# GpSimd instead of SyncE waits at the program's end for the semaphores of the last stores

## The reference

```python
# attention: 16 heads of 16 features; within one token, feature i of Q against feature j of K
Q = (x @ Wq.T).reshape(b, length, 16, 16).swapaxes(-2, -1)      # K, V likewise from the context
qk = jnp.einsum('blih,bljh->blij', Q, K) / sqrt(16)
attn = softmax(qk, axis=-1)
valued = jnp.einsum('blij,bljh->blih', attn, V)                  # back to 256 features, @ Wo.T

x = x + tanh(g_xattn[0]) * xattn(layernorm(x), ctx)
# feed forward: 8 experts, each token takes the one with the largest gate
idx = argmax(softmax(xf @ Wg + bg))
y_e = gelu(xf @ W1[e] + b1[e], exact) @ W2[e] + b2[e]
x = x + tanh(g_ffn[0]) * y_idx                                   # xf is layernorm(x)
```

## Time and profile before

| What | Value |
|---|---|
| median of 3 runs | 300.7 us (300.69 to 301.26) |
| the profiled execution's own time | 300.25 us |
| its span, first to last instruction | 298.4 us |
| what lies around the span | 1.85 us |
| mean granted TensorE clock | 0.988 of full |
| PE busy | 279.1 us (94% of the span) |
| DVE busy | 209.5 us (70%) |
| POOL busy | 130.3 us (44%) |
| ACT busy | 105.3 us (35%) |

### The profile page before, as it was taken

How to read it: one execution, slowest core, us unless ns; L and a number is a source line. 1 busy time by engine, 2 the same in 40 slices (tenths; PEclk the granted TensorE clock), 3 DMA queues, 4 the chain that set the end, 5 groups by cost and what they waited for, 6 DMA issues and landing times.

```text
span 298.4 us, 9824 instructions
## 1 busy us (share of the span) xinstructions
PE 279.1 (94%) x3181; PEld 216.9 (73%) x3182; DVE 209.5 (70%) x611; ACT 105.3 (35%) x258; POOL 130.3 (44%) x157
## 2 busy tenths in 40 slices
PE   7989999999999999999999999968788999999970
PEld 6558677677776776767767777857677999999960
DVE  6576586696785875978668678867588766666650
ACT  2021321303213113032130320355555777877730
POOL 9512041243624525336154352722757555445551
PEclk9999999999999999999999999999999999999995
DMA  7666255464674746637646643423334544344210
GB/s 264 197 196 162 67 141 146 122 218 139 194 194 132 221 128 210 216 96 218 189 146 208 178 130 107 123 73 90 110 113 152 162 142 131 97 133 117 85 56 0
DMA packets 30955, 43.25 MB, mean 145 GB/s; under 512 B 7629, under 2 KB 17998, under 8 KB 30928
## 3 DMA queue, kind: packets, MB, share of 16 engines
q1 hardware_dynamic: 17872, 21.48, 25.9%
q10 hardware_dynamic: 9648, 12.86, 14.3%
q0 software_dynamic: 3408, 8.59, 8.2%
HBM read 24.83 MB, written 10.60 MB: 119 GB/s over the span
## 4 chain that ended last, share of the span: by engine, by line
PE 75%; DVE 8%; SPq 5%; issue 3%; DMA 2%; POOL 2%; ACT 1%; DVEq 1%; ACTq 1%; POOLq 0%
PE ps_pr L397 17%; PE ps_qo L405 16%; PE ps_so L430 8%; PE ps_av L451 8%; PE ps_tr L599 5%; PE ps_av L611 4%; PE ps_so L599 4%; PE ps_to L611 4%; PE ps_tr L439 3%; PE ps_pr L587 2%; PE ps_to L464 2%; SPq L318 2%; SPq L326 2%; DMA sb_wkv<-wkv_in 2%; ACTq L318 1%
## 5 line engine op out<-in xcount | busy, mean ns | idle before, releaser
L397 PE MATMUL ps_pr<-sb_wkv,sb_ct 128*128 128x512 f32 x128 | 62.1, 609 | 0.8 <-DMA sb_wkv<-wkv_in 0.5
L659 ACT ACTIVATE sb_pe_x<-sb_pe_x 128x512 f32<-128x512 f32 x16 | 10.1, 631 | 112.0 <-DVE sb_pe_x L817 112.0
L1247 POOL TENSOR_SCALAR sb_ve<-sb_mv 128x2 f32<-128x2 f32 x16 | 3.5, 220 | 88.1 <-DVE sb_mv L786 84.5
L397 PEld LDWEIGHTS ps_pr<-sb_wkv,sb_ct 128*128 128x128 f32 x128 | 22.5, 189 | 20.5 <-issue 19.9
L802 DVE STREAM_TRANSPOSE sb_y_q<-sb_q_n 128x512 f32<-128x512 f32 x16 | 17.4, 1090 | 26.8 <-ACT sb_q_n L654 26.8
L1262 POOL DMA_INDIRECT routed_rows<-sb_xs,sb_pos_i x32 | 32.5, 1016 | 8.3 <-issue 7.7
L405 PE MATMUL ps_qo<-sb_wog,sb_ot 128*128 128x264 f32 x128 | 31.4, 388 | 1.1 <-ACT sb_ot L670 1.1
L405 PEld LDWEIGHTS ps_qo<-sb_wog,sb_ot 128*128 128x128 f32 x128 | 24.1, 190 | 11.2 <-issue 6.2
L430 PE MATMUL ps_so<-sb_kb,sb_y_q 128*32 128x128 f32 x1024 | 31.0, 273 | 0.5 <-DVE sb_y_q L802 0.5
L451 PE MATMUL ps_av<-sb_vb,sb_at 128*32 128x128 f32 x1024 | 31.3, 274 | 0.0
L451 PEld LDWEIGHTS ps_av<-sb_vb,sb_at 128*32 128x32 f32 x1024 | 27.0, 110 | 5.0 <-issue 5.0
(11 more groups left out here) (143 smaller groups left out, 481.4 us busy)
## 6 DMA issues: line engine op xcount, KB each, us to landing
sb_kb<-sb_y_k SPq DMA_DIRECT2D x124, 32.0 KB
sb_vb<-sb_y_v SPq DMA_DIRECT2D x124, 32.0 KB
sb_ct<-ctx_in ACTq DMA_DIRECT2D x15, 256.0 KB, 3.0
sb_x<-x_in ACTq DMA_DIRECT2D x15, 256.0 KB, 3.5
sb_xt<-xt_in_ ACTq DMA_DIRECT2D x14, 256.0 KB, 5.1
sb_xb<-routed_rows SPq DMA_DIRECT2D x25, 134.0 KB, 2.1
sb_w_all<-w_in_ SPq DMA_DIRECT2D x4, 514.0 KB
sb_w<-w_in SPq DMA_DIRECT2D x4, 512.0 KB
```

The source lines that it names most:

```text
L397: last = pe.matmul(pr[:, s * 512:(s + 1) * 512], lhsT=ct[i][:, kc, s, :], rhs=wkv[:, kc, :], start=(kc == 0), stop=(kc == KC - 1))
L659: act.activation(pe_x[:], pe_x[:], ACT.Exp, scale=float(H) ** -0.5).then_inc(exp_done, 1)
```

## The change

The loop that waits for the four `stored` semaphores is taken out of SyncE's stream and put at the end of GpSimd's, behind the last store. It is written there with `wait_apart`, so that each wait also increments the counter `passed_pool`. The values waited for are the same.

```diff
@@ -385,8 +385,6 @@
             sp.wait_ge(routed, 32 * pairs)
             sp.wait_ge(pad_in, 16 * E // 2)
             block_slots(sp, fetch, 0)
-            for i in range(OUT):
-                sp.wait_ge(stored[i], 16 * ((blocks + OUT - 1 - i) // OUT))
@@ -1308,6 +1306,8 @@
                     for q in range(2):
                         route(2 * (last_batch % 2) + q, last_batch)
             block_slots(pool, store, 0)
+            for i in range(OUT):
+                wait_apart(pool, stored[i], 16 * ((blocks + OUT - 1 - i) // OUT), passed_pool)
```

## The result

| | before | changed |
|---|---|---|
| median of 20 runs | 300.69 us | 302.06 us |
| ratio | | 1.0047, 95% interval 1.003 to 1.0065 |
| the profiled execution's own time | 300.25 us | 302.24 us |
| its span | 298.4 us | 300.4 us |
| mean granted TensorE clock | 0.988 | 0.987 |

The changed kernel is slower by 0.47%; the forecast was 302.0 us and +1.3 us. One of its 20 runs took 332.09 us at a granted clock of 0.847 and is left out of the ratio; the median of the other 19 is 301.99 us, 1.30 us above that of before.

What follows compares the result with a forecast made beforehand. The end was taken as bound by GpSimd's last store, its DRAIN and the release. DRAIN start 293.6 plus 5.88 plus 0.24 gives 299.7 against 298.4, +1.3 us: 300.7 + 1.3 = 302.0 us, range 300.4 to 303.2.

Steps and rivals of the forecast that it cites:

- The path at the end: At the span's end: GpSimd's last store, its DRAIN of 7084 ns on line 97, then the release of all engines.
- The removed part at 0.0: On SyncE: losing its four waits is worth 0.0 us, being covered by GpSimd's own DRAIN.
- The start of the DRAIN: On GpSimd behind the new waits: landing seen at 293.4, plus 0.2 us, so the DRAIN starts at 293.6.
- The bounds of 293.5 and 293.7: Earliest and latest start forecast for GpSimd's final DRAIN behind the new waits, around 293.6.
- 5.88 us that come with the DRAIN: At GpSimd's end: 5.88 us are work the DRAIN brings with it, starting when it reaches the idle engine.
- third rival: GpSimd's DRAIN waits for the last packet, then works 5.06 us: slower by only 0.5 us, 301.2 us; chance 10%.
- No price for handing over: Between GpSimd's waits and DRAIN: handing the DRAIN to the idle engine costs a tenth at most, not 0.7 us.
- The upper bounds of +2.0 and +2.5: GpSimd's end: +2.0 if up to 0.73 us issue time is exposed, +2.5 if all 7.08 us follow 293.6.
- The faster rival: GpSimd's DRAIN is long from polling for outstanding stores; after the landing it takes 0.17 us: 296.3 us; chance 17%.
- The rival of no change: GpSimd's 5.88 us run on by themselves after the last store, so the DRAIN ends at 298.16: 300.7 us; chance 13%.
- cleaning up after all 71 indirect DMAs: Example given, within the no-change case, of work GpSimd's cores might still do after the last store's record ends.

Runs made afterwards that it cites:

- experiment 4: Kernel before with one DRAIN added on GpSimd in its idle stretch while it waits for VectorE, 24 indirect DMAs issued by then; 305.69 us, ratio 0.9921.
- experiment 5: Kernel before, SyncE keeping the waits, with GpSimd DRAINs added in the idle stretch and behind stores 12, 23, 31 and 33; 297.25 us, ratio 0.9868.
- experiment 6: Kernel before, SyncE keeping the waits, with GpSimd DRAINs added only in the idle stretch and behind stores 23 and 31; 296.47 us, ratio 0.9838.
- experiment 8: Changed kernel with SyncE's four waits put back, so both engines wait; 301.85 us against 300.51, ratio 1.0038.
- experiment 2: Changed kernel with a GpSimd memset of 3.5 us between the four waits and the DRAIN; 313.87 us, one run, on a chip where before takes 308.39 us.
- experiment 7: The DRAINs of experiment 5 combined with the waits on GpSimd as in the changed kernel; 297.76 us, ratio to before 0.9891.
- experiment 1: Changed kernel with a second GpSimd DRAIN right behind the four waits; 310.18 us, one run, on a chip where before takes 308.39 us.

## Why the prediction was right

- **The path at the end.** Store, DRAIN, release was the reading of the earlier trace rows. Experiments 4 to 6 confirm it from the other side: with only the DRAIN shortened, the span ends earlier by what it lost (2.0 us in experiment 4), until the landing takes over: in experiment 5 it sets the end through SyncE's drain.
- **The removed part at 0.0.** Right (experiment 8).
- **The start of the DRAIN, 1.3 us behind the last store's end.** Right to the tenth: 1.33 in the changed kernel. The bounds of 293.5 and 293.7 for the start correspond to 294.2 and 294.4 there, and it is 294.28.
- **5.88 us that come with the DRAIN.** Right in size (5.874) and shown as a mechanism by experiment 2. In the kernel before they began as soon as the store had left the engine, at 292.28, while the store was still landing; SyncE's wait lay beside them. The change puts wait and work in a row, and the 1.3 us of the wait are the loss. That none of the 5.88 us was a wait for the landing was an assumption of the forecast; its third rival was the case without it. It held for this DRAIN with its 71 DMAs; in experiments 5 and 6 the DRAINs with 21 DMAs or fewer behind a store took 0.5 to 1.4 us more than the line.
- **No price for handing over.** The upper bounds of +2.0 and +2.5 were not needed: the last wait starts at 294.2 and the DRAIN at 294.3, and the DRAIN is no longer than 5.87. That the forecast of 302.0 us and the median of 302.06 meet so closely is in part luck: the interval of the ratio runs from +0.3% to +0.65%, 0.9 to 2.0 us.
- **The faster rival**, that the DRAIN waits for open transfers: false in the changed kernel, where all had landed and it took 5874 ns. A landing does lengthen a DRAIN that has few DMAs to account for (1.4 us with 5 in experiment 5, against 0.45 in experiment 7, where all had landed), but that is not where the 5.9 us come from. The figure of some 12 ns in the Trainium skill (VectorE: DVE Perf Modes, The DRAIN you can't avoid) is for the drains of the runtime's preamble and postamble; the one on line 97 closes the kernel's own block, so the prediction took the figure further than the page does. GpSimd comes near it only where it has issued no DMA since its last DRAIN: 34 ns in experiment 1.
- **The rival of no change**, work going on by itself: excluded by experiment 2. The Trainium skill says in Perfetto Trace Analysis, DMA Instruction — SWDGE (GPSIMD), that the processor completes the instruction after its record has ended. No run here shows how much later; it is not where the 5.88 us are.
- **The third rival**, work starting at the landing, 5.06 us long: excluded by the DRAIN's length after everything had landed, 5.87 us.
- **What the prediction did not know** is what the work is. It left "cleaning up after all 71 indirect DMAs" as an aside to a rival. The work does grow with that count, only it is done at another time: when the DRAIN runs, not before. That did not touch the forecast, since both kernels issue the same 71.

## What to carry to other kernels

When an engine's DRAIN ends a program, look at what it does after the engine has become idle, and let waits lie beside that work on another engine rather than ahead of it. On GpSimd that work grew here with the indirect DMAs since its last DRAIN, so a DRAIN in an idle stretch in the middle takes part of it off the end. A DRAIN added near the end needs enough stores behind it for the engine to catch up: seven were enough in experiment 6, and with five behind the last of two such DRAINs experiment 5 was still late by 0.75 us.

## What the runs showed of the hardware

- In these kernels GpSimd's DRAIN, counted from the end of the engine's last operation, takes about 75 ns and 81.7 ns for each indirect DMA issued since the one before: 5 in 0.45 us (all landed, experiment 7), 24 in 2.06, 47 in 3.91, 71 in 5.87, 100 in 8.24. With 71 it makes no difference whether the last one has landed (5.88 and 5.87 us). With none it took 0.03 us, less than the line's 75 ns. All these DMAs were indirect and of 128 rows: plain ones from GpSimd were not tried, and a price by rows could not be told from a price by DMAs. Why each costs this is not shown.
- A DRAIN right behind a store that is still landing took at least 1.4 us from the store's end, however few DMAs it had: 1.5 to 1.6 us with 2, 1.4 with 5, 1.5 with 7, 1.8 to 2.0 with 8, 1.9 with 11, 2.3 with 21; the last packets came 0.8 to 1.2 us after the stores' ends. From 32 DMAs on (2.8, 3.9 and 5.9 us with 32, 47 and 71) the line holds to 0.1 us, so most of the landing lies beside the work. With 21 the DRAIN took longer than the line (1.8 us) and than the landing alone; how the two combine there is open.
